# Attention over a full adjacency on one core: both halves of the exchange issued by SyncE, the second group's layer norm split between VectorE and ScalarE, and the setup's calls reordered

## What is computed

```python
h = maximum(layernorm(x), 0)                 # x: 4096 x 256, f32
q, k, v = h @ Wq.T + bq, h @ Wk.T + bk, h @ Wv.T + bv
a = q @ k.T / 16 + adj + adj                 # 4096 x 4096
out = x + softmax(a, axis=-1) @ v
```

## Time and profile before

| | us |
|---|---|
| three runs: median (lowest to highest) | 712.77 (710.68 to 718.14) |
| the profiled execution's own time | 712.38 |
| its span | 710.6 |
| TensorE busy in it | 689.6 (97%) |
| VectorE / ScalarE / POOL busy | 581.3 / 431.6 / 427.6 |

### The profile page before, as it was taken

One profiled execution on the slowest core, in us unless ns is written; L12 is line 12 of the kernel. 1 busy time (PEld: TensorE's weight loads), 2 busy tenths in 40 slices (PEclk: granted clock), 3 DMA queues, 4 the chain that ended last, 5 costly groups with the idle time before them and its releaser, 6 DMA issues.

```text
span 710.6 us, 14184 instructions
## 1 busy us (share of the span) xinstructions
PE 689.6 (97%) x4799; PEld 475.1 (67%) x4799; DVE 581.3 (82%) x1284; ACT 431.6 (61%) x732; POOL 427.6 (60%) x434
## 2 busy tenths in 40 slices
PE   5789999999999999999999999999999999999998
PEld 4556546676666666766766676667666667666786
DVE  4899788888888888788888888797877878887897
ACT  4899564756755675657576565746566665656440
POOL 1879506564754665665657474656637575655587
PEclk9999999999999999999999999999999999999999
DMA  8558699999999999999989898989998899988572
GB/s 267 172 161 263 169 249 302 267 234 245 216 225 240 242 250 203 261 224 266 232 239 236 215 249 237 249 229 234 211 253 222 243 230 228 249 234 211 127 208 68
DMA packets 85048, 160.99 MB, mean 227 GB/s; under 512 B 12784, under 2 KB 33648, under 8 KB 84976
## 3 DMA queue, kind: packets, MB, share of 16 engines
q1 hardware_dynamic: 64336, 126.39, 69.7%
q10 hardware_dynamic: 20640, 33.70, 20.1%
HBM read 80.35 MB, written 8.39 MB: 125 GB/s over the span
## 4 chain that ended last, share of the span: by engine, by line
PE 74%; DMA 13%; ACT 3%; SPq 3%; DVE 2%; issue 2%; POOL 1%; ACTq 1%; DVEq 0%; POOLq 0%
PE bank L1457 42%; PE bank L1524 32%; DMA xT<-rows 4%; DMA out_y<-xy 3%; DMA rows<-in_adj 3%; ACT rows L723 1%; DMA xy<-in_x 1%; PE bank L1471 1%; DMA rows<-in_x 1%; DMA g_scratch<-xT 1%; SPq L436 1%; SPq L426 1%; SPq L407 1%; ACTq L801 1%; DMA v_sb<-rows 1%
## 5 line engine op out<-in xcount | busy, mean ns | idle before, releaser
L641 POOL TENSOR_TENSOR wT<-xT,wT 128x512 f16<-128x512 f32 x233 | 267.4, 1163 | 191.0 <-ACT wT L818 190.9
L1457 PE MATMUL bank<-v_sb,wT 128*128 128x256 f16 x2796 | 342.6, 273 | 0.0
L1524 PE MATMUL bank<-top,a_op 128*128 128x512 f16 x1344 | 331.1, 379 | 3.3 <-DVE rows L1089 1.4
L1457 PEld LDWEIGHTS bank<-v_sb,wT 128*128 128x128 f16 x2796 | 273.6, 98 | 80.5
L818 ACT CAST wT<-xT 128x512 f16<-128x512 f32 x233 | 139.1, 611 | 141.8 <-DVE rows L1138 129.3
L1524 PEld LDWEIGHTS bank<-top,a_op 128*128 128x128 f16 x1344 | 130.8, 98 | 112.7 <-DVE rows L1096 3.1
L1111 DVE CUSTOM_DVE_ANT_0 rows<-bank,rows 128x512 f32<-128x512 f32 x256 | 173.7, 680 | 12.1 <-PE bank L1524 3.4
L792 ACT ACTIVATE rows<-rows,exp_bias,exp_scale 128x1024 f32<-128x1024 f32 x128 | 158.3, 1237 | 35.8 <-DVE exp_bias L1178 29.1
L1138 DVE STREAM_TRANSPOSE rows<-rows 128x1024 f32<-128x1024 f32 x128 | 158.4, 1239 | 0.2 <-ACT rows L792 0.2
L1096 DVE SCALAR_TENSOR_TENSOR rows<-rows,adj_scale,bank 128x512 f32<-128x512 f32 x64 | 47.8, 746 | 53.5 <-PE bank L1524 53.5
L1089 DVE SCALAR_TENSOR_TENSOR rows<-rows,adj_scale,bank 128x512 f32<-128x512 f32 x64 | 47.6, 744 | 27.8 <-PE bank L1524 20.9
(11 more groups left out here) (115 smaller groups left out, 452.7 us busy)
## 6 DMA issues: line engine op xcount, KB each, us to landing
rows<-in_adj SPq DMA_DIRECT2D x128, 512.0 KB, 8.1
xT<-rows SPq DMA_DIRECT2D x244, 128.0 KB, 4.2
xT<-rows ACTq DMA_DIRECT2D x244, 128.0 KB, 6.5
rows<-in_x SPq DMA_DIRECT2D x8, 512.0 KB, 6.0
xy<-in_x SPq DMA_DIRECT2D x32, 128.0 KB, 4.8
g_scratch<-xT SPq DMA_DIRECT2D x16, 256.0 KB, 4.6
g_pair<-g_scratch SPq DMA_DIRECT2D x15, 256.0 KB, 5.0
out_y<-xy SPq DMA_DIRECT2D x30, 128.0 KB, 7.9
```

Of the source, the lines that this page charges most:

```text
L641: nc.gpsimd.tensor_tensor(split_piece(m, 1), exchanged(m), split_piece(m, 0), ALU.subtract).then_inc(split_lo, 1)
L1457: return nc.tensor.matmul(out_ap, stationary, moving, start=first, stop=last)
L1524: last = nc.tensor.matmul(ps[:], s, mv, start=first and k == 0, stop=k == 2, skip_group_check=True)
```

## The change

Three edits.

1. **Exchange.** SyncE gets an `exchange_b(u)` with all four DMAs of the second half, called in the setup for units 0 to 2 and in every period up to n = 63; ScalarE's calls go, but for the last units (u = 60 and later). SyncE's period has another order, and the refill of a unit's first row moves from the period after the exchange into the same one.
2. **Group 1.** ScalarE's four `normalise(1, k)` go. VectorE scales and shifts (`normalise_second`, four `tensor_scalar` 128x256 f32), TensorE transposes that, ScalarE's two `copy_h(1, c)` become ReLU activations.
3. **Order of the setup.** The lists of calls of all five engines are permuted; B11 of q = 0 goes from VectorE to POOL, T3 of q = 0 and T2 of q = 1 from POOL to VectorE, B22 of q = 3 from VectorE to POOL. `statistics(1)` stands behind the first `tensor_reduce` into `tops`.

```diff
+            def exchange_b(u):
+                sp.wait_ge(turned, 2 * u + 2)
+                arrival_free(sp, u)
+                for i in range(P // Q):
+                    sp.dma_start(arrivals(u)[2 * Q:P, i].rearrange("p j q -> p (j q)"),
+                                 unit_row(u, 1)[i * Q:(i + 1) * Q, :]).then_inc(landing(u, 1), 16)
...
             exchange_a(0)
             store_g(4)
+            exchange_b(0)
             refill(0, 0)
...
             refill(0, 1)
             exchange_a(1)
+            exchange_b(1)
             exchange_a(2)
             refill(1, 0)
+            exchange_b(2)
             refill(1, 1)
+            refill(2, 0)

             def period(n):
                 p, u = n // QUADS, n - EXP_LAG
                 if n % QUADS == 0 and p >= 3:
                     store(2 * (p - 3) + 1)
+                if n % QUADS == 3 and p >= 2:
+                    store(2 * (p - 2))
                 if unit_in_range(u):
                     exchange_a(u)
+                if unit_in_range(u - 1):
+                    refill(u - 1, 1)
                 if n % QUADS in (0, 1) and 2 <= p < PAIRS:
                     load_xy(2 * p + n % QUADS)
                 if n % QUADS == 0 and p + 1 < PAIRS:
                     load_g(p + 1)
-                if unit_in_range(u - 1):
-                    refill(u - 1, 0)
-                if unit_in_range(u - 1):
-                    refill(u - 1, 1)
-                if n % QUADS == 3 and p >= 2:
-                    store(2 * (p - 2))
+                if unit_in_range(u) and n < PERIODS:
+                    exchange_b(u)
+                if unit_in_range(u):
+                    refill(u, 0)
...
+            def normalise_second():
+                slot = 1 % len(X_UNITS)
+                dve.wait_ge(ln_done, 2)
+                for k in range(KT):
+                    t = KT + k
+                    last = nc.vector.tensor_scalar(x_ring[slot][:, k, :], x_ring[slot][:, k, :],
+                                                   ln_all[:, 0, t:t + 1], ln_all[:, 1, t:t + 1],
+                                                   ALU.mult, ALU.add)
+                last.then_inc(h1_done, 1)
...
-            statistics(1)
             dve.wait_ge(m_done, 1)
             nc.vector.tensor_reduce(tops[:, 0:1], bank[1][:], AX.X, ALU.max,
                                     apply_absolute_value=True)
+            statistics(1)
...
                                     ).then_inc(tops_reduced, 1)
+            normalise_second()
             dve.wait_ge(tops_shared, 1)
...
-            low_key(0, B11)
...
```

More of the change, by code:

```diff
@@ L489, in _ @@
             load_rows(11)
+            store_g(1)
+            low_keys(sp, 2, B11, B21, B22)
+            sp.wait_ge(t_made, 12)
+            load_rows(12)
+            move_v(3)
             move_v(4)
@@ L830, in _ @@
             normalise(0, 3)
-            normalise(1, 0)
             copy_h(0, 0)
+            copy_h(0, 1)
+            high_key(0, B21)
+            copy_h(1, 0)
             high_key(0, B11)
-            copy_h(0, 1)
-            normalise(1, 1)
-            normalise(1, 2)
-            high_key(0, B21)
-            normalise(1, 3)
+            copy_h(1, 1)
             act.wait_ge(scales_done, 1)
@@ L1635, in _ @@
             last.then_inc(small_done, 1)
+            project_g(0, 0)
             project_v(0)
-            project_g(0, 0)
             project_g(0, 1)
-            project_v(1)
             transpose_h(2, 0)
             transpose_h(2, 1)
-            project_g(1, 0)
+            project_v(1)
             project_v(2)
             transpose_h(3, 0)
+            transpose_h(3, 1)
+            project_g(1, 0)
+            product_2(0)
             project_v(3)
-            transpose_h(3, 1)
+            product_5(0)
             transpose_h(4, 0)
```

290 lines of the change are left out of this document (134 added, 156 removed).

## The result

| | before | after |
|---|---|---|
| median (lowest to highest, runs) | 712.88 us (710.68 to 718.14, 4) | 753.82 us (741.25 to 759.19, 4) |
| profiled execution: own time / span | 712.38 / 710.6 us | 741.25 / 739.5 us |
| TensorE busy / not busy in the span | 689.6 / 21.0 us | 697.7 / 41.8 us |

The ratio is 1.0445, with a 95% interval of 1.0306 to 1.0584: the change makes the kernel slower by 3 to 6%, where 709.3 us and "same" were forecast. The profiled execution is the fastest of the four, so the trace shows 28.9 of the 41 us: 20.8 us more in which TensorE has no matmul, and 8.1 us more in which it has one.

A forecast was written before the change was run, and what follows sets the result against it. TensorE was taken to bound the kernel, with at most 21.0 us of idle to win. 712.38 - 0.8 (setup walk) - 0.8 (later waits up to 74 us) - 1.5 (row waits) = 709.3 us, range 705.5 to 714.

The forecast's parts named there:

- The exchange: SyncE's steady period: 6.7 us of issue in 9.78, 2.6 us to spare in the median; cost 0, steady waits go, -1.2 us.
- (3): SyncE becomes the bound at the wait in refill(u, 0): 28 us less some 12 us of cover, 728 us; chance 0.08.
- ScalarE's relief: Steady part: ScalarE loses four issues a period, but TensorE doesn't wait for it there, so worth 0.
- One queue carries the traffic: SyncE's queue alone: it moves 341 to 419 GB/s between 60 and 85 us, so it carries 240; cost 0.
- The walk: Setup call by call: group 1 transposed 1.7 us earlier, half given back by group 2; -0.8 us, bounds -2.5 and +1.0.
- the 1.6 I had summed: Setup lead: 0.8 us left at group 4's transposes, and 0.8 us from a third of later waits up to 74 us.
- rival (1): End of the setup gives the lead back, SyncE having twelve more DMAs, 7 us of issue: 712 to 713 us; chance 0.16.
- The -1.5 us for row waits: TensorE's waits for late row loads go: -1.2 us in the steady part, -0.3 at the setup's end; bounds -1.5 and +0.5.

The follow-up runs named there:

- e14: Changed kernel, with both refills of unit u - 1 ahead of exchange_a(u), then exchange_b(u) and the loads of x rows and g: 776.9 us, ratio 1.083.
- e13: Changed kernel, with refill(u - 1, 0) ahead of the loads and exchange_b(u), and refill(u - 1, 1) behind them: 768.3 us, ratio 1.069.
- e8: Changed kernel, with only exchange_b(u) moved directly behind exchange_a(u): 717.3 us, ratio 1.002 to the kernel before.
- e5: Changed kernel, with only refill(u - 1, 1) moved from ahead of the loads to behind exchange_b(u): 719.0 us, ratio 1.004 to the kernel before.
- e10: Changed kernel, with exchange_b(u) directly behind exchange_a(u), then the loads, then both refills of unit u - 1: 715.8 us, ratio 0.998.
- e12: Setup of the kernel before; from unit 2 SyncE issues exchange_a, exchange_b, loads, then both refills of unit u - 1: 716.1 us, ratio 1.000.
- e2: Changed kernel, with both refills, now of unit u - 1, last in SyncE's period, behind the loads and exchange_b(u): 719.1 us, ratio 1.006.
- e1: Changed setup with the steady part of the kernel before, exchange_b there back on ScalarE: 715.4 us, ratio 0.999.
- e6: Changed kernel, with only the first row's refill put back to the next period, ahead of refill(u - 1, 1): 740.8 us (718 to 744), no ratio.
- e15: Changed kernel, with loads first, then exchange_a(u), refill(u - 1, 0), exchange_b(u), refill(u - 1, 1): 730.3 us, ratio 1.020.
- e16: Changed kernel, with only the loads of x rows and g moved ahead of exchange_a(u): 774.4 us, ratio 1.071 to the kernel before.
- e9: Changed kernel, with refill(u - 2, 1) for refill(u - 1, 1) and refill(u - 1, 0) for refill(u, 0), each in the same place: 754.4 us, ratio 1.049.
- e7: Setup of the kernel before; from unit 2 SyncE issues exchange_a, loads, exchange_b, then both refills of unit u - 1: 717.0 us, ratio 1.002.

## Why the prediction was wrong

**The step that failed** is the one on SyncE's loop, under "The exchange": "One wait in it is new in kind: `refill(u, 0)` stands behind the landing of the exchange_a(u) issued in the same period", with "2.6 us to spare in the median". Two things are wrong in it. First, a second wait is new in kind: `refill(u - 1, 1)`, which I entered as 0.5 us of issue, had stood behind loads and now stands ahead of exchange_b(u) while it waits for the landing of exchange_b(u - 1). I never drew that loop. Second, the landing: I used 4.2 us, the median of the first half. With 4.2 plus 2.5 to 4 us of issue this loop would have closed in time too; but it is the second half that closes it, and that half's own row read 6.5 us, which gives 9.0 to 10.5 us against a period of 9.78. It measured 5.9 us in the median of its DMAs and 6.5 to 7.5 us from the last of them on the chain, and with 7.4 the loop is 9.9 us and more. The runs show that either suspect costs alone: e14, the loop with the halves together, has a landing of 4.9 us and a time of 776.9; e13, late landings without the loop, has 768.3. e8, one call moved, takes both away and has 3.2 us and 717.3. How the changed kernel's 41 us divide between the two no run shows.

**The rival.** (3), "SyncE becomes the bound", named the mechanism and got 0.08, with its price of 728 us. Its place was wrong: the wait in `refill(u, 0)` is still there in e5 and e8, at 719.0 and 717.3 us. Its size was too small: 28 us less some 12 us of cover, where the median rose by 41. The four rounds shown run 0.33 us a period late, which over 57 periods is 19 us and near the 20.8 us of lost TensorE time in the traced, fastest execution, so no cover shows in it; the median is 12.6 us above that execution. And I left out that TensorE's matmuls themselves took longer, 8.1 us in all, at a mean granted clock of 0.98 where it had been 1.00. The range, 705.5 to 714, left all of this out.

**Steps that held.** ScalarE's relief is worth nothing in the steady part (e10, e12: 0.998 and 1.000 with all of b on SyncE). One queue carries the traffic: 235 to 237 GB/s in e2, e8 and e10 on SyncE's queue alone, 236 on two before. The Trainium skill, "DMA: Bandwidth & Descriptors", section "Issuing engines are not separate DMA queues", says that a second issuing engine only saves the time of issue; these runs agree, at 717.3 (e8) and 715.8 us (e10) against 716.7 and 716.8 for the kernel before. What moved with the DMAs here is their place among SyncE's waits: the same calls on the same queue took 717.3 us in e8 and 753.8 in the changed kernel.

**The setup.** The walk was right to a tenth in most places (timeline of PE, changed kernel):

```profile
16.39 1.97 PE L1478 MATMUL bank<-ident,rows 128*128 128x128 f32 x8 [0.54 <-DVE rows L1066]
...
28.56 1.10 PE L1478 MATMUL bank<-ident,rows 128*128 128x128 f32 x8 [1.88 <-ACT rows L738]
...
32.52 0.50 PE L1461 MATMUL bank<-xT,top 128*128 128x256 f16 x3 [1.55 <-DVE rows L1082]
...
37.52 0.81 PE L1531 MATMUL bank<-top,a_op 128*128 128x512 f16 x3
...
40.12 0.60 PE L1478 MATMUL bank<-ident,rows 128*128 128x128 f32 x4
...
110.88 1.47 PE L1461 MATMUL bank<-v_sb,wT 128*128 128x256 f16 x12
...
124.50 1.47 PE L1531 MATMUL bank<-top,a_op 128*128 128x512 f16 x6 [2.38 <-DVE rows L1092]
```

Group 1 was forecast for 16.5, group 2 for 28.55 (but behind an idle of 3.75 us, which was 1.88: TensorE came to it later, on the slower clock told of below, and ScalarE set the time either way), project_v(2) for 32.5, product_2(0) for 37.5, group 4 for 40.1. The weighing starts at 110.88; before it was 112.05, a lead of 1.2 us for the 1.6 I had summed. And then it is given back, at 124.50, as rival (1) said: that rival was the right one for this part, and e1 (0.999) and e10 beside e12 (715.8 and 716.1 us) show no worth of the setup's edits that can be measured. The -1.5 us for row waits didn't come either: from 120 us on TensorE still waits 8.3 us for rows in e2 and 3.1 us in e10.

**What stays open.** How much of the changed kernel's loss is the loop and how much the later landings. Whether r0's wait adds to it (e6). Why the packets take longer when row loads lie between the halves (below). What of e15's remaining 14 us comes from late rows (TensorE waits 12.4 us for them) and what from late exchanges. How the loss divides in the changed kernel's slower executions, at 750 to 759 us, was not traced.

## What to carry to other kernels

When a DMA call is moved to an engine that works through a list in order, draw each landing wait of that list with the call that it releases, and look for a ring: landing, wait, next issue of the same kind. Its length is one landing plus the issues between, and it has to be compared with the period by the landing that the new order will give, not by the old one; where the two are within a few us, put the wait behind the next issue (here one moved call, 754 to 717 us). The engine with the longest wait in the list need not be the path: moving its loads forward (e16) changed its wait from 163 to 54 us and did not shorten the time. A better sign of the ring is the issuer's slack: SyncE's wait for VectorE ahead of exchange_a was 153.3 us before, 107.4 in e10, 13.5 in the changed kernel and 8.7 in e14.

## What the runs showed of the hardware that was not expected

**Packets took longer where row loads lay between the halves.** The kernels with both halves on SyncE throughout move 157.86 MB on one queue. Its packets take 83.4% of 718.1 us = 599 us in e2, 577 in e8 (80.6% of 715.9) and 600 in e10 (84.3% of 712.2), with the halves' DMAs together; 688 us in the changed kernel, 706 in e13 and 694 in e15, with a 512 KB row load between them. The landing goes from 3.2 to 3.5 us to 5.8 to 7.8 us. The order isn't all of it: e14, halves together but behind two row loads, has 633 us and a landing of 4.9, and e1, with the period of before, has 687 us on its two queues together where the kernel before had 638, in traces of 721 and 712 us. A queue served in ring order, as the Trainium skill has it ("DMA: Bandwidth & Descriptors", section "Queues, rings and completion order"), would make the half behind a row load land later, by about 512 KB at 237 GB/s = 2.2 us (an estimate from e10's table). In e9 the second half takes 6.1 us and the first 4.4, which is near it; in the changed kernel they take 5.9 and 5.6, which that order doesn't explain. Why the packets themselves take 15% longer no run here shows.

**TensorE's clock in the first 30 us.** In the traced execution of the changed kernel the granted clock is 0.53 between 10 and 20 us and 0.79 between 20 and 30, that is partly at the 1.2 GHz level; before it was 1.00. This isn't the change's doing: it differs from execution to execution. Nine of the eighteen traces have 0.53 to 0.60 between 10 and 20 us and nine have 1.00, and both setups are among each: e12 (0.53) and e7 (1.00) have the setup of before, the changed kernel (0.53) and e16 (1.00) the same new one. In the nine with the low clock TensorE had been idle 2.8 to 3.2 us ahead of the first transposes of the rows (3.04 us ahead of 13.15 in the changed kernel), in the nine others 1.5 to 1.9 us. In the changed kernel:

```profile
10.00:20.00 10.00, 6.42 (x25) 5.25 (x24) 6.95 (x33) 6.33 (x13) 3.41 (x6) 0.53 0.99 357
20.00:30.00 10.00, 8.07 (x42) 4.91 (x42) 9.48 (x37) 7.38 (x17) 8.79 (x9) 0.79 0.41 151
```

It cost nothing here: the next thing was a wait for ScalarE, 1.88 us long at the slow clock and 3.48 us in e10, which has the same setup up to there and a clock of 1.00. Group 1 was transposed 0.55 us later than in e10 (16.39 and 15.84) and group 2 0.56 us later (28.56 and 28.00), so nothing was added between them.
